# A cross-attention and mixture-of-experts block on one core: buffers of 512 bytes or more begin at multiples of 128 bytes instead of 64

## The chip, the cores and the metric

The kernel runs on one core of a Trainium2 chip. The metric is the device time of one execution in microseconds (us). Each time is the median of several executions. The profile is of one execution, taken by the hardware profiler.

## The reference

The kernel computes a transformer block on x (64 sequences of 64 tokens, 256 features) with a context of the same shape.

```python
x = x + jnp.tanh(g_xattn[0]) * attention(_layernorm(x), ctx_2048, Wq, Wk, Wv, Wo, ...)
x = x + jnp.tanh(g_ffn[0]) * experts(_layernorm(x), w_router, w_gate, w_up, w_down, ...)
```

The attention has 16 query heads and 4 key and value heads of 128, RMS norm and rotary embedding on queries and keys, and keys and values from the 64 context tokens and the 64 own tokens of each sequence. The expert part has a shared expert of width 352, and 8 experts of width 176 of which each token takes the best two by a softmax router, scaled by 2.5.

## The kernel before

**Stages.** The 4096 tokens are 32 tiles of 128 (two sequences each). After an opening of some 49 us (sine and cosine tables, weight loads), attention runs over 128 steps, one for each tile and each of the 4 key and value heads. The steps are staggered by hand: in the step that computes the scores of (tile, head) n, TensorE also projects queries and keys for n + 2 (b_q, L1697, and b_kv, L1711), transposes queries and keys of n (b_qT, b_kT, L1754 and L1758), transposes the softmax of n - 1 (b_pT, L1777), multiplies it by the values (b_aT, L1784) and applies the output projection to n - 2 (b_o, L1795). Then come 71 slots of 128 rows, sorted by expert (L1998 to L2052), and last the shared expert for tiles 8 to 31 (L1828, L1940, L1946). Tiles 0 to 7 of the shared expert run between attention and the slots.

**Matmuls.** The projections and the experts run in fp32r, one pass over the moving columns for each matmul, three matmuls for one product (high by high, high by low, low by high; the tables PASSES and the names _hi and _lo). Scores, values and transposes run in f32. In the profile's names a group b_kv<-w_group,kv_in_hi writes b_kv, streams w_group and holds kv_in_hi as the stationary operand. A b_kv group is 12 matmuls of 256 columns, a b_o group 12 of 256, a b_q group 6 of 512, a gate or up projection 6 of 352, a down projection of the shared expert 9 of 256 and one of a slot 5 of 256.

**Order of the work.** Each engine has its own program, with semaphores between them. ScalarE (ACT) and VectorE (DVE) empty the PSUM banks and write the high and low parts, GpSimd (POOL) does part of the norms and the rotary embedding, SyncE (SP) issues nearly all transfers.

**Memory.** All SBUF buffers are placed by hand. The helper `sb` keeps a cursor in bytes per partition, places a buffer there and moves the cursor on by the size rounded up to 64. With an `at` argument it places the buffer over older ones, from a cursor of its own. The first buffer is at byte 16,512. Rings used in turn matter below: `yS0` to `yS7` hold the normed tokens of shared-expert tile t in yS[t % 8], where tiles 8 and later write their gate to b_q and their up projection to b_kT; `s_in0` to `s_in3` hold a slot's rows, of which 0 and 2 are transposed into b_kT and 1 and 3 into b_o; `s_silu0` is computed from b_q and `s_silu1` from b_kv; `w2_new0` and `w2_new1` are stored to memory in turn. Of the eight chunks sincos0 to sincos7, ScalarE's final steps (L912 to L914) come in the order 0, 4, 1, 5, 2, 6, 3, 7.

Of the kernel before, what the change touches and what calls it, by code (L numbers as in the profile page):

```python
# [63 lines left out]
PI_BELOW = 3.1415925  # L64
PASSES = ((0, 0), (0, 1), (1, 0))
HI, LO = 0, 1

def need(eng, sem, count):
# [28 lines left out]
def flamingo(nc, x, ctxT, posx, posc, invf, g_xattn, g_ffn, q_w, k_w, wq, wkv, wo, wr, wg, wd, out):  # L98
    ctx = ExitStack()
    with ctx:  # L100
# [3 lines left out]
        def sb(name, shape, dt, at=None):  # L104
            size = int(np.prod(shape[1:])) * mybir.dt.size(dt)
            where = cursor if at is None else at
            t = nc.alloc_sbuf_tensor_at(name, shape, dt, offset=where[0])
            where[0] += -(-size // 64) * 64
            return t

        def parts(name, shape, at=None):
            return [sb(f"{name}_{p}", shape, F32R, at) for p in ("hi", "lo")]

        ident = sb("ident", [P, P], F32)
        gates = sb("gates", [P, 2], F32)
        gates_raw = sb("gates_raw", [P, 2], F32)
        minus_half = sb("minus_half", [P, 8], F32)
# [2033 lines left out]
```

How the kernel before makes its waits and increments, by code:

```python
def need(eng, sem, count):  # L69
    if not isinstance(count, int) or count > 0:
        eng.wait_ge(sem, count)
# [346 lines left out]
            def load_inputs(t, p):  # L419
                need(sp, x_normed, t - 1)
                sp.dma_start(x_in[p][:], x[bass.ds(t, 1), :, :].rearrange("a p n -> p (a n)")).then_inc(ld_x[p], 16)
                if isinstance(t, int) and t == 2:
                    sp.wait_ge(ctx_hi, 1)
                need(sp, ctx_lo, t - 2)
                sp.dma_start(ctx_raw[p][:], ctxT[bass.ds(t, 1), :, :, :].rearrange("a p c n -> p (a c) n")) \
                  .then_inc(ld_ctx[p], 16)
# [47 lines left out]
            def load_yS(t):  # L475
                i, r = divmod(t, RING // 2)
                if t >= RING:
                    sp.wait_ge(up_done, t - RING + 1)
                elif t >= RING // 2:
                    sp.wait_ge(q_done, 4 * TILES)
                    sp.wait_ge(kv_done, 4 * TILES)
                need(sp, ld_yS[r], 16 * i)
                sp.wait_ge(st_yT, 16 * (t + 1))
                sp.dma_start(yS_both[t % RING][:].rearrange("p a c n -> p (a c n)").bitcast(F32),
                             yT_dram[t, :, :]).then_inc(ld_yS[r], 16)
# [1 line left out]
            def load_x1_first():  # L487
                for p in range(2):
                    sp.wait_ge(st_x1[p], 16 * (PAIRS - 1))
                for n, (read, times) in enumerate(((x_normed, TILES), (ctx_lo, TILES - 1))):
                    sp.wait_ge(read, times)
# [1185 lines left out]
        @block.tensor  # L1678
        def _(pe):
            pe.wait_ge(consts_set, 9)
```

## Time and profile before

| what | value |
|---|---|
| median of 3 executions | 1233.44 us |
| lowest and highest | 1232.87 and 1234.34 us |
| the profiled execution | 1232.5 us |
| its span (first to last instruction) | 1230.7 us |
| granted TensorE clock, mean | 0.999 of full speed |

In the views, PE is TensorE's matmul, PEld its weight loads (which overlap), DVE VectorE, ACT ScalarE, POOL GpSimd, and SPq the transfers that SyncE issues. The chain is the work that ended last, followed back from the last instruction to what released each step. In order of time, each of its pieces has a start, a length that counts the piece's share of the chain, and a number of instructions, so that the length over the number is the pace at which they follow one another. The duration of one matmul in other views is longer than that, since matmuls are pipelined.

### The profile page before, as it was taken

The page shows a single profiled execution, that of the slowest core. Times are in us where ns is not written, and L with a number is a line of the kernel's source. Part 1 is how long each engine was busy: PE and PEld are TensorE (multiplying, and loading weights), DVE is VectorE, ACT ScalarE, POOL GpSimd, SP SyncE. Part 2 cuts the span into 40 slices and gives each one's busy share as a digit, 9 for nine tenths or more (in the row PEclk, how much of TensorE's full clock was granted, in tenths as well). Part 3 has the DMA queues.
Part 4 walks back from the last instruction along what each step waited for, and adds up shares of the span by engine and source line. Part 5 has one row for each costly group of instructions (what it writes and reads, how often), then busy time and mean ns, then how long its engine had stood idle before and what let it go on. Part 6 is the DMA issues. An engine that isn't in the chain of part 4 may idle for free.

```text
span 1230.7 us, 31490 instructions
## 1 busy us (share of the span) xinstructions
PE 1205.3 (98%) x8781; PEld 1137.3 (92%) x8782; DVE 1008.7 (82%) x2992; ACT 884.9 (72%) x3754; POOL 922.4 (75%) x1124
## 2 busy tenths in 40 slices
PE   6899999999999999999999999999999999999998
PEld 3688999999999999999999999999999999999997
DVE  8788888888888888888888888888888677777443
ACT  7978777777777777777777777777777546666322
POOL 2778888888888888888888888888887425556654
PEclk9999999999999999999999999999999999999999
DMA  6634233322222222223333333222236536554575
GB/s 179 198 115 128 72 111 106 100 90 90 90 90 90 94 90 94 90 90 93 115 108 99 103 103 120 94 75 75 75 110 213 193 104 188 163 158 150 186 230 158
DMA packets 128792, 148.57 MB, mean 121 GB/s; under 512 B 13824, under 2 KB 108288, under 8 KB 127968
## 3 DMA queue, kind: packets, MB, share of 16 engines
q1 hardware_dynamic: 122256, 130.16, 34.8%
q0 software_dynamic: 6480, 17.77, 4.0%
q8 instruction: 22, 0.36, 0.1%
q14 instruction: 34, 0.28, 0.1%
HBM read 66.93 MB, written 80.76 MB: 120 GB/s over the span
## 4 chain that ended last, share of the span: by engine, by line
PE 94%; DVE 2%; ACT 2%; issue 1%; DMA 0%; SPq 0%; DVEq 0%
PE b_kv L1711 14%; PE b_q L1697 14%; PE b_o L1795 13%; PE b_sc L1769 9%; PE b_aT L1784 9%; PE b_pT L1777 5%; PE b_qT L1758 4%; PE b_q L2031 3%; PE b_kv L2031 3%; PE b_q L1828 2%; PE b_kT L1754 2%; PE b_kT L1828 2%; PE b_aT L1946 1%; PE b_aT L2048 1%; PE b_pT L2048 1%; PE b_o L1747 1%
## 5 line engine op out<-in xcount | busy, mean ns | idle before, releaser
L1711 PE MATMUL b_kv<-w_group,kv_in_hi 128*128 128x256 f32 x992 | 205.6, 305 | 0.0
L957 ACT ACTIVATE probs<-b_sc,neg_max 128x128 f32<-128x128 f32 x512 | 180.5, 372 | 0.1
L747 POOL TENSOR_TENSOR qk_r<-qk_me,minus_half 128x6 f32<-128x6 f32 x128 | 172.8, 1350 | 10.1
L751 POOL TENSOR_TENSOR q_rot<-q_rot,q_sin 128x512 f32<-128x512 f32 x128 | 164.4, 1284 | 6.7 <-DVE q_sin L1273 1.9
L1711 PEld LDWEIGHTS b_kv<-w_group,kv_in_hi 128*128 128x128 f32 x992 | 161.8, 190 | 6.7 <-issue 0.4
L1697 PE MATMUL b_q<-w_group,kv_in_hi 128*128 128x512 f32 x496 | 164.8, 413 | 0.0
L951 ACT ACTIVATE pT<-b_pT 128x512 f32<-128x512 f32 x128 | 76.7, 600 | 99.7 <-PE b_pT L1777 97.7
L1795 PE MATMUL b_o<-wo_hi,aT_hi 128*128 128x256 f32 x480 | 143.5, 299 | 0.1
L1769 PE MATMUL b_sc<-kT,qT 128*128 128x128 f32 x1024 | 135.9, 275 | 6.8 <-ACT qT L946 4.9
L754 POOL TENSOR_TENSOR q_rot<-q_rot,qk_r 128x512 f32<-128x512 f32 x128 | 133.7, 1044 | 10.0
L1711 PE MATMUL b_kv<-w_group,kv_in_lo 128*128 128x256 f32 x496 | 139.6, 282 | 0.0
L940 ACT ACTIVATE junk<-b_q 128x128 bf16<-128x128 f32 x512 | 133.9, 283 | 0.0
L1769 PEld LDWEIGHTS b_sc<-kT,qT 128*128 128x128 f32 x1024 | 124.7, 191 | 9.0 <-issue 8.1
L1795 PE MATMUL b_o<-wo_lo,aT_hi 128*128 128x256 f32 x480 | 133.0, 277 | 0.0
L1795 PE MATMUL b_o<-wo_hi,aT_lo 128*128 128x256 f32 x480 | 132.7, 276 | 0.0
L1784 PE MATMUL b_aT<-pT,v 128*128 128x256 f32 x512 | 131.4, 379 | 0.0
L745 POOL TENSOR_TENSOR qk_me<-qk_ms,eps_rms 128x6 f32<-128x6 f32 x128 | 32.2, 252 | 119.0 <-ACT junk L928 118.7
L1283 DVE TENSOR_REDUCE neg_max<-b_sc 128x4 f32<-128x512 f32 x128 | 88.3, 690 | 36.6 <-PE b_sc L1769 34.7
L1784 PEld LDWEIGHTS b_aT<-pT,v 128*128 128x128 f32 x512 | 96.5, 189 | 17.5 <-issue 0.5
L940 ACT ACTIVATION_READ_ACCUMULATOR junk<-b_q 128x1 f32 x512 | 111.2, 217 | 0.0
L957 ACT ACTIVATION_READ_ACCUMULATOR probs<-b_sc,neg_max 128x1 f32 x512 | 109.1, 213 | 0.0
L760 POOL TENSOR_TENSOR k_rot<-k_rot,k_sin 128x256 f32<-128x256 f32 x128 | 93.6, 731 | 11.4 <-DVE k_sin L1259 8.8
(309 smaller groups left out, 3937.5 us busy)
## 6 DMA issues: line engine op xcount, KB each, us to landing
xs_scratch<-zeros SPq DMA_DIRECT2D x34, 1032.0 KB, 6.3
s_in<-xs_scratch SPq DMA_DIRECT2D x71, 129.0 KB
yT_scratch<-yT SPq DMA_DIRECT2D x32, 256.0 KB
yS<-yT_scratch SPq DMA_DIRECT2D x32, 256.0 KB, 3.0
routed<-ys_scratch SPq DMA_DIRECT2D x32, 256.0 KB, 3.5
w_hi_all<-w_scratch SPq DMA_DIRECT2D x3, 1536.0 KB, 13.6
x_in<-in_x SPq DMA_DIRECT2D x32, 128.0 KB, 2.3
ctx_raw<-in_ctxT SPq DMA_DIRECT2D x32, 128.0 KB, 2.5
```

The lines of the kernel that those rows point to most:

```text
L747: nc.gpsimd.tensor_tensor(qk_r[g % 2][:], qk_me[:], minus_half[:, 0:REP + NB], ALU.pow).then_inc(r_ready, 1)
L751: nc.gpsimd.tensor_tensor(q_rot[g % 2][:], q_rot[g % 2][:], q_sin[g % 2][:], ALU.add) \
L754: nc.gpsimd.tensor_tensor(q_rot[g % 2][:], q_rot[g % 2][:], qk_r[g % 2][:, 0:REP].unsqueeze(2).to_broadcast([P, REP, HD]), ALU.mult) \
L760: nc.gpsimd.tensor_tensor(k_rot[g % 2][:], k_rot[g % 2][:], k_sin[g % 2][:], ALU.add) \
L940: last = nc.scalar.activation(junk[:, h, :], b_q[:, h * HD:(h + 1) * HD], ACT.Square, scale=HD ** -0.5, accum_out=qk_ms[g % 2][:, h:h + 1])
L957: last = nc.scalar.activation(probs[:, j, :], b_sc[:, j * P:(j + 1) * P], ACT.Exp, bias=neg_max[g % 2][:, j:j + 1], accum_out=row_sum[g % ...
L1283: nc.vector.tensor_reduce(neg_max[g % 2][:], b_sc[:].rearrange("p (j n) -> p j n", j=REP), AX.X, ALU.max, negate=True).then_inc(max_ready, 1)
L1697: last = nc.tensor.matmul(b_q[:], kv_in[p][a][:, c, 1:3, :], wq_of(b, gg)[:, c, :], start=(c == 0 and (a, b) == PASSES[0]), stop=(c == DC ...
L1711: last = nc.tensor.matmul(b_kv[:, s * 2 * HD:(s + 1) * 2 * HD], kv_in[p][a][:, c, 2 * s:2 * s + 2, :], wkv_of(b, c)[:, g % KVH, :], start= ...
L1769: last = nc.tensor.matmul(b_sc[:, o:o + P], qT[:, s, 2 * j:2 * j + 2, :], kT[:, s, :], start=True, stop=True)
L1784: last = nc.tensor.matmul(b_aT[:, s * REP * S:(s + 1) * REP * S], v_s[g % KVH][:, s, :], pT[:, s, :], start=True, stop=True)
L1795: last = nc.tensor.matmul(b_o[:, 0:D], aT[a][:, h, :, :], wo_s[b][:, gg * REP + h, :], start=(gg == 0 and h == 0 and (a, b) == PASSES[0]), ...
```

## The change

```
+WIDE, LINE = 512, 128
...
             size = int(np.prod(shape[1:])) * mybir.dt.size(dt)
             where = cursor if at is None else at
+            if size >= WIDE:
+                where[0] = -(-where[0] // LINE) * LINE
             t = nc.alloc_sbuf_tensor_at(name, shape, dt, offset=where[0])
             where[0] += -(-size // 64) * 64
```

A buffer of 512 bytes or more per partition first rounds its cursor up to a multiple of 128. The first that this moves is wg_raw, at 18,240. The addresses below follow from the sizes, in the order of the calls of `sb` (bytes; in brackets the rest modulo 128):

| buffers | before | after |
|---|---|---|
| ident | 16,512 (0) | 16,512 (0) |
| wr (128 bytes) | 18,112 (64) | 18,112 (64) |
| wg_raw, wg_lo, wq_raw | 18,240 (64) | 18,304 (0) |
| wd_raw, wd_lo | 46,400 (64) | 46,464 (0) |
| w_group, w2_hi_all | 65,856 (64) | 65,920 (0) |
| sincos2 | 59,456 (64) | 59,520 (0) |
| wo_hi, x1_most / wo_lo | 115,008 / 131,392 (64) | 115,072 / 131,456 (0) |
| hid0 to hT1_lo | 150,592 to 158,272 (64) | 150,656 to 158,336 (0) |
| x_in, x_res, x1_out, x_n | 160,064 to 168,256 (64) | 160,128 to 168,320 (0) |
| s_silu0 / s_silu1 | 164,160 (64) / 164,864 (0) | 164,224 (0) / 164,992 (0) |
| kv_in0_hi to kv_in1_lo, yS4 to yS7 | 169,280 to 175,424 (64) | 169,344 to 175,488 (0) |
| s_in0, s_in2 | 177,472, 179,648 (64) | 177,536, 179,840 (0) |
| s_in1, s_in3 | 178,560, 180,736 (0) | 178,688, 180,992 (0) |
| q_rot0 to v3, qT, kT, probs, pT | 179,328 to 200,832 (0) | 128 more (0) |
| sT, s_hid, s_hT, s_out | 181,824 to 195,136 (64) | 320 more (0) |
| sincos0, sincos4 | 195,712, 199,808 (0) | 128 more (0) |
| aT_hi, aT_lo | 202,880, 204,928 (0) | 203,008, 205,056 (0) |
| y_row0 / y_row1 | 207,360 (0) / 209,472 (64) | 207,488 (0) / 209,664 (0) |
| yT0, yT1 | 211,584, 213,632 (0) | 256 more (0) |
| w2_new0, w2_new1, yS0 to yS3 | 219,648 to 225,792 (0) | 384 more (0) |

All slices of the weights that a matmul streams are whole multiples of 128 bytes from their buffer's start, and so are the stationary slices. The last byte used goes from 227,840 to 228,224 (229,368 are there).

## Rows read from the trace of the kernel before

**Rows 1.** The page: busy time, share and instructions of each engine.
```profile
PE 1205.3 (98%) x8781; PEld 1137.3 (92%) x8782; DVE 1008.7 (82%) x2992; ACT 884.9 (72%) x3754; POOL 922.4 (75%) x1124
```

**Rows 2.** Busy us in windows: PE, PEld, DVE, ACT, POOL, clock, transfers.
```profile
0.00:49.00 49.00, 33.65 (x123) 20.35 (x125) 38.57 (x79) 41.37 (x122) 20.81 (x41) 1.00 0.80 236
49.00:1143.00 1094.00, 1089.77 (x8075) 1035.84 (x8074) 933.52 (x2839) 819.12 (x3583) 852.19 (x1017) 1.00 0.35 109
500.00:909.00 409.00, 409.00 (x3064) 388.35 (x3064) 358.39 (x1020) 316.93 (x1467) 345.87 (x394) 1.00 0.30 94
1143.00:1230.70 87.70, 81.93 (x588) 81.15 (x586) 36.56 (x76) 24.45 (x52) 49.45 (x67) 0.98 0.62 199
```

**Rows 3.** The page: the chain that ended last, shares of the span.
```profile
PE 94%; DVE 2%; ACT 2%; issue 1%; DMA 0%; SPq 0%; DVEq 0%
```

**Rows 4.** The chain in order of time, one step of attention.
```profile
601.04 1.37 PE b_o L1795 x12
602.42 0.89 PE b_sc L1769 x8
...
603.96 1.38 PE b_q L1697 x6
605.34 0.86 PE b_aT L1784 x4
606.21 1.43 PE b_kv L1711 x12
```

**Rows 5.** Single buffers: operations on s_silu, y_row and s_in, ns min/median/max.
```profile
L1118 ACT ACTIVATE s_silu<-b_q x36: 309/318/347, 999.2 to 1141.8; 128x176 f32<-128x176 f32 x36
L1118 ACT ACTIVATE s_silu<-b_kv x35: 310/318/318, 1001.8 to 1139.8; 128x176 f32<-128x176 f32 x35
...
L1322 DVE TENSOR_SCALAR y_row<-x_out,ln_mv,ln_rstd x32: 536/539/558, 79.0 to 980.5; 128x512 f32<-128x512 f32 x32
L1998 PE MATMUL b_kT<-ident,s_in x72: 270/272/273, 996.2 to 1137.8; 128*128 128x128 f32 x72
L1998 PE MATMUL b_o<-ident,s_in x70: 271/272/273, 997.9 to 1135.5; 128*128 128x128 f32 x70
```

**Rows 6.** The chain in order of time, the closing stage.
```profile
1142.00 0.36 PE b_aT L2048 x3
...
1146.85 0.96 PE b_q L1828 x6
1147.81 0.96 PE b_kT L1828 x6
1148.78 1.08 PE b_sc L1946 x9
...
1156.84 0.97 PE b_q L1828 x6
1157.81 0.95 PE b_kT L1828 x6
...
1166.84 0.97 PE b_q L1828 x6
```

**Rows 7.** ScalarE in order of time, the opening.
```profile
15.10 0.71 ACT L914 ACTIVATE sincos<-sincos,half_pi 128x512 f32<-128x512 f32 x1
...
25.03 0.70 ACT L914 ACTIVATE sincos<-sincos,half_pi 128x512 f32<-128x512 f32 x1
```

**Rows 8.** Waits: who for whom, us in total, times, longest.
```profile
POOL qk_me L745 <- ACT junk L928: 118.7, 67, 15.8
...
PE b_sc L1769 <- ACT qT L946: 4.9, 3, 2.5
```

**Rows 9.** Landing of w2_new's stores (100 to 200 us), then of the output tiles' stores.
```profile
DMA to landing us min/median/max: 2.3/2.3/2.3
DMA to landing us min/median/max: 1.7/2.1/4.0
```

**Rows 10.** The page: groups of b_kv and b_o matmuls, with counts.
```profile
L1711 PE MATMUL b_kv<-w_group,kv_in_hi 128*128 128x256 f32 x992 | 205.6, 305 | 0.0
...
L1795 PE MATMUL b_o<-wo_hi,aT_hi 128*128 128x256 f32 x480 | 143.5, 299 | 0.1
```

More of the change, by code:

```diff
@@ L66 @@
 HI, LO = 0, 1
+WIDE, LINE = 512, 128
 def need(eng, sem, count):
@@ L106, in sb @@
             where = cursor if at is None else at
+            if size >= WIDE:
+                where[0] = -(-where[0] // LINE) * LINE
             t = nc.alloc_sbuf_tensor_at(name, shape, dt, offset=where[0])
```

## The prediction

> **What bounds the kernel now.** I read the busy shares first [rows 1], then the busy time in windows [rows 2], then the chain of work that ended last, as a share by line [rows 3] and in order of time [rows 4, 6], and the list of waits [rows 8]. The reader is to see one engine. TensorE is busy for 1205.3 of 1230.7 us [rows 1]. In windows it is idle for 15.4 us of the first 49 us, for 5.8 us of the last 88 us, and for 4.2 us in all of the 1094 us between [rows 2]. The chain is 94% TensorE and 0% DMA [rows 3]. The long wait totals in [rows 8] belong to GpSimd, ScalarE and VectorE, which wait for TensorE or for each other with slack; the longest of TensorE's own that I show is 4.9 us over three times. So a change of memory addresses can move the time only if (a) it changes how fast TensorE's matmuls and weight loads follow one another, or (b) it changes the ScalarE and VectorE work in the first 49 us. Nothing else is worth more than a few tenths of a microsecond.
>
> **What the change does.** It adds and removes no instruction, wait or transfer. It moves addresses (the table in the section on the change): the weights, the kv_in ring, the trig tables, hT, sT and s_hT go from 64 bytes past a multiple of 128 ("phase 64" below) to phase 0. What was at phase 0 already (ident, q_rot, qT, kT, v, probs, pT, aT, yT, yS0 to yS3, s_in1, s_in3, s_silu1, the w2_new pair) stays at phase 0 and moves by whole multiples of 128, or not at all. So the kernel before already runs both phases side by side, and its trace holds the comparison.
>
> **Part 1: ScalarE and VectorE, and the first 49 us.** s_silu0 is at phase 64 and fed from b_q, s_silu1 at phase 0 from b_kv. ScalarE's write takes 318 ns in both [rows 5]. For VectorE, the row on y_row covers y_row0 (phase 0) and y_row1 (phase 64) together, and its 32 instructions spread from 536 ns to 539 (median) to 558 [rows 5]: half of them could not be off by more than 22 ns. In the opening, ScalarE's last step for chunk 2 of sincos, at phase 64, takes 0.70 us at 25.03, and that for chunk 4, at phase 0, takes 0.71 us at 15.10 [rows 7]. Taken at zero. The bounds: 0.01 us less or more on each of a few sincos steps that are on the chain, below 0.1 us either way. GpSimd shows no pair of phases that I can separate. In [rows 2] it has slack in every stage (345.9 busy of 409 us in the second half of attention), and no wait of TensorE for it is among the long ones [rows 8], so it is hidden behind TensorE's queue of work; if it lost all slack, that would need 18% on every one of its instructions.
>
> **Part 2: transposes and f32 matmuls.** The 72 transposes of s_in0 and s_in2 (phase 64, into b_kT) and the 70 of s_in1 and s_in3 (phase 0, into b_o) both take 272 ns [rows 5]. The cost is zero for these and, by them, for the other transposes whose input moves (x_n, y_row1, hid, s_hid). Scores, values and the transposes of attention have both operands at phase 0 before and after.
>
> **Part 3: the fp32r matmuls.** These carry the chain, and here one comparison is missing: every fp32r moving operand (w_group, wo, w2_hi_all, wg_lo, wd_lo; wr too, which is too small to be moved) is at phase 64 before, so no row shows one at phase 0. The stationary operand does come in both phases. In the closing stage each token tile of the shared expert reads yS[t % 8]: t = 9 to 11 read yS1 to yS3 (phase 0), t = 12 to 15 read yS4 to yS7 (phase 64). A tile starts every 3.33 us in both. Its two groups of six take 0.96 + 0.96 us at phase 0 and 0.97 + 0.95 us at phase 64: the sum is 1.92 in both [rows 6]. Three tiles take 9.99 us (1146.85 to 1156.84) and the next three 10.00. The split between the two groups does shift by 0.01 us, so addresses are visible to TensorE, but the sum is not: 0.1% of the stage. Taken over the whole kernel, that is at most 1.2 us either way.
>
> What disturbs this is that two groups of identical form do not run alike. The twelve matmuls of b_kv (kv_in at phase 64 against w_group at 64) take 1.43 us, 119 ns each. The twelve of b_o (aT at phase 0 against wo at 64) take 1.37 us, 114 ns each [rows 4]. Both have 128x256 moving and 128x128 stationary. The nine of the shared down projection (hT at 64, wd at 64) take 1.08 us, 120 ns each, in a stage where ScalarE and VectorE do little [rows 2, 6], so it isn't traffic from those that slows them. Something in the addresses makes 5 ns. Phase is one candidate. A higher address bit is another: every fp32r moving operand of the groups at 119 to 120 ns lies below byte 115,008 of the partition, both halves of wo lie above it, and no buffer changes sides by being moved 64 to 384 bytes. The yS comparison argues for the second, as it shows no effect of phase; but it is at 352 columns. My value is zero; the ends are the two rivals.
>
> **What a rule would make of it.** The Trainium skill ("SBUF — State Buffer", on the DMA port swizzle) says that SBUF works in lines of 16 bytes and that only a change of line costs; 64 is a multiple of 16, so by that rule all phases are alike and the sum is zero. It doesn't explain the 114 against 119 ns, so I don't rest on it.
>
> **Part 4: transfers.** Stores of w2_new alternate between a buffer at a multiple of 256 and one at 128 past it, and land in 2.3 us, minimum, median and maximum alike [rows 9]. x1_out, x1_most and s_out go from 64 to 128 past a multiple of 256. None of these is waited for except the last output tile, which lands in about 2 us [rows 9] after the last VectorE step. By that rule the last store would be 6% slower in its transfer part, an estimate of 0.1 us if all of its 2.1 us were that; the trace has no such difference between 0 and 128 past. Taken at zero from the rows.
>
> **The sum.** 0 (part 1) + 0 (part 2) + 0 (part 3) + 0 (part 4). The profiled execution took 1232.5 us, 1.8 of it outside the span; the median of three runs is 1233.44, and the sum is made to that: 1233.4 us.
>
> **Rivals.**
> *Faster, phase of the stationary operand.* If phase 0 is what gives aT its 114 ns, then kv_in, hT and s_hT gain it: 1488 matmuls of b_kv (992 that hold kv_in_hi [rows 10], and half as many that hold kv_in_lo) by 5 ns (7.4 us); 32 x 9 = 288 of the shared down projection and 71 x 5 = 355 of the slots' (0.36 us for the first three [rows 6], 120 ns each) by 6 ns (3.9 us). Sum 11.3 us, 1222.1 us. For it: four families agree. Against it: yS. Its far end is that the moving operand at phase 64 is the cause and every fp32r matmul reaches the column rate of the f32 ones: 0.86 us for four of 256 columns with two passes [rows 4], 107.5 ns a pass, or the 111 ns of the b_sc pairs (0.89 us for 8) where weight loads bound it. That gives 744 x (230 - 215) = 11.2 us for b_q (124 groups of 6, 1.38 us each [rows 4]), 12.2 for b_kv, 4.6 for b_o, 810 x 12 = 9.7 for the 352-column ones (0.96 or 0.97 us for six, 160 ns, against 148), 5.8 for down: 43.5 us, 1190 us. Nothing speaks for it but that it hasn't been seen.
> *Slower, phases that meet.* If a matmul is slow where stationary and moving operand have the same phase, b_kv, hT and s_hT are slow for that and b_o is fast because aT (0) and wo (64) differ. The change puts both at 0. Then 1440 matmuls of b_o (three times 480 [rows 10]) go from 114 to 119 ns: 7.2 us, 1240.6 us. It decides from 1.7 ns a matmul on (0.2%). For it: the same four families, equally well. Against it: yS0 to yS3 against w2 differ in phase, yS4 to yS7 do not, and both cost 1.92 us.
> *No effect, since it doesn't do what it says.* It does move the buffers: the first one of 512 bytes after the small ones is at 18,240, and 18,240 is 142.5 x 128. This isn't apart from the forecast in time.
>
> **How the numbers follow.** Forecast (zero, with up to 1.2 us of re-timing either way): 0.64, own range 1231 to 1236. Stationary phase: 0.14, 1222. Full column rate: 0.03, 1190. Phases that meet: 0.14, 1241. Something unseen: 0.05, split between the sides. A measurement of this kernel can tell about 0.2% (2.5 us) from no change. The range of 8 in 10 takes the forecast and the rival on the slow side, and part of the way to the fast one: 1224 to 1242. Of the forecast's 0.64, 0.03 lies beyond 2.5 us on each side. Faster 0.14 + 0.03 + 0.02 + 0.03 = 0.22; slower 0.14 + 0.03 + 0.03 = 0.20; same 0.58.
>
> **What would show it.** In the changed kernel's trace: b_kv groups of 12 still at 1.43 us, b_o groups at 1.37, b_q groups of 6 at 1.38, down projections at 1.08 for nine, shared tiles every 3.33 us. A b_o group at 1.43 shows that phases that meet are the cause; b_kv at 1.37 and down at 1.03 show the stationary phase; b_q at 1.29 the full rate. I'm wrong if any of these groups moves by 0.03 us or more, since attention has 120 to 124 of each, or if TensorE gets waits that [rows 8] don't have.

## The result and the profile after

The changed kernel takes 1238.15 us (median of 8, 1237.34 to 1239.27) where the kernel before took 1233.59 us (median of 8, 1232.41 to 1234.44) beside it: slower by 4.6 us, ratio 1.0037 with a 95% interval of 1.0027 to 1.0048. The profiled execution took 1238.04 us with a span of 1236.3 us, 5.6 us longer than the span before. The diff adds three lines, so line n of the kernel before is line n + 3 here.

The page of the changed kernel first: busy times of the engines and the chain's shares, to be read beside [rows 1] and [rows 3].

```profile
PE 1211.1 (98%) x8781; PEld 1142.7 (92%) x8782; DVE 1007.2 (81%) x2992; ACT 884.2 (72%) x3754; POOL 918.1 (74%) x1124
...
PE 93%; DVE 2%; ACT 2%; DMA 1%; issue 1%; SPq 0%; POOL 0%; DVEq 0%; POOLq 0%
```

TensorE is busy for 5.8 us more with the same 8781 matmuls; the three other engines are busy for slightly less. So no other engine's own work got longer: the matmuls themselves take longer. The granted clock isn't the cause. It is 1.00 in attention, as it was before [rows 2] (window in us, then PE, PEld, DVE, ACT, POOL, clock, transfers):

```profile
110.00:977.00 867.00, 863.85 (x6413) 818.45 (x6412) 749.25 (x2132) 664.74 (x3069) 715.74 (x818) 1.00 0.33 103
```

The waits hardly change. The three longest of TensorE's waits in the changed kernel (us in total, times, longest):

```profile
PE b_kT L1688 <- DVE x_n L1238: 8.3, 2, 8.0
PE b_sc L1772 <- ACT qT L949: 4.4, 3, 2.5
PE b_kT L1757 <- POOL k_rot L763: 2.4, 2, 1.8
```

The first was 8.3 us before too, and the second 4.9 us [rows 8]. The third was one wait of 1.9 us before; the second wait in it, of 0.6 us, is new. Next, where in the execution it happens: the first and last start of the matmuls of the output projection, then of the transposes of the slots. First the kernel before, then the changed one (duration of one in ns, min/median/max, then the starts in us).

```profile
L1795 PE MATMUL b_o<-wo_lo,aT_hi x480: 276/276/283, 110.0 to 977.5; 128*128 128x256 f32 x160
```

```profile
L1798 PE MATMUL b_o<-wo_lo,aT_hi x480: 278/282/287, 110.1 to 983.7; 128*128 128x256 f32 x160
L2001 PE MATMUL b_kT<-ident,s_in x72: 270/273/273, 1002.5 to 1143.7; 128*128 128x128 f32 x72
```

At 110 us the two kernels are level. At the last output projection the changed one is 6.2 us late (983.7 against 977.5), at the first slot 6.3 us (1002.5 against 996.2 [rows 5]), at the last slot transpose 5.9 us, and at the end 5.6 us. The loss is made in attention, but not all of it by the pace. The lateness grows at an even rate until 958 us (on the clock of the kernel before), from 0.1 to 5.5 us. Right after that comes the new wait of 0.6 us: TensorE waits for GpSimd's k_rot, which comes after a long transfer. Two pieces of the chain of the changed kernel there (start, length, in us):

```profile
961.69 6.89 DMA xs_scratch<-y_row,row_i
968.64 0.92 POOL k_rot L763
```

About as much is given back in the slots, so at the end the lateness is what the even growth had made. The same wait of 0.6 us stands in one of the runs below in which every pace is that of before (all_plus_64). So it doesn't come from the pace of the matmuls.

One step of attention, in the chain of the changed kernel (start, length, both in us), beside [rows 4]:

```profile
604.16 1.42 PE b_o L1798 x12
605.58 0.89 PE b_sc L1772 x8
...
607.13 1.40 PE b_q L1700 x6
608.52 0.86 PE b_aT L1787 x4
609.39 1.43 PE b_kv L1714 x12
```

b_o went from 1.37 to 1.42 us, b_q from 1.38 to 1.40. b_kv, b_sc and b_aT stand where they stood. From the starts of the matmuls in all groups, the median time from a b_o group's first start to the next group's is 1458 ns before and 1501 after, and for b_q 1468 and 1478 ns: 43 and 10 ns a group. b_o's 43 ns aren't in every group: 12 of the 120 were already longer before, and little or nothing is added to them. Summed over the groups up to 958 us, b_o adds 4.5 us, b_q 1.3 and b_kv -0.1, together 5.6 us, beside the 5.4 us by which the lateness grows there. The timeline shows the pace. First a b_o group's second half before, then after (starts in us):

```profile
608.71 0.28 PE L1795 MATMUL b_o<-wo_hi,aT_lo 128*128 128x256 f32 x1
...
609.39 0.28 PE L1795 MATMUL b_o<-wo_hi,aT_lo 128*128 128x256 f32 x1
```

```profile
604.59 0.29 PE L1798 MATMUL b_o<-wo_hi,aT_lo 128*128 128x256 f32 x1
...
605.30 0.28 PE L1798 MATMUL b_o<-wo_hi,aT_lo 128*128 128x256 f32 x1
```

Six matmuls take 0.68 us before and 0.71 after. Over all groups this pace (twelfth start less sixth, by six) is 113.3 ns before, in every one of the 120 groups, and 119.4 ns on average after, with none of the 120 groups near 113. In b_kv it is 119.4 before and 119.2 after, with none of 124 groups near 113 in either. This measure, a group's pace, is worked out from the starts in the trace, and the experiments below are read by it.

The closing stage, now that yS0 to yS7 and w2 are all at multiples of 128, in the chain of the changed kernel:

```profile
1155.67 0.96 PE b_q L1831 x6
1156.63 0.95 PE b_kT L1831 x6
1157.58 1.08 PE b_kv L1949 x9
...
1158.99 0.97 PE b_q L1831 x6
```

The second b_q row starts 3.32 us after the first. A tile starts every 3.32 to 3.33 us through this stage, as before the change [rows 6].

### The profile page after: what moved, and what is told of

It reads as the page before. It is cut to its first block, busy times and chain, and to the rows that moved or that the text cites. A ratio compares the mean times of both kernels' runs of the same rounds, so it can differ in the third digit from the quotient of the medians.

```text
span 1236.3 us, 31490 instructions
## 1 busy us (share of the span) xinstructions
PE 1211.1 (98%) x8781; PEld 1142.7 (92%) x8782; DVE 1007.2 (81%) x2992; ACT 884.2 (72%) x3754; POOL 918.1 (74%) x1124
## 4 chain that ended last, share of the span: by engine, by line
PE 93%; DVE 2%; ACT 2%; DMA 1%; issue 1%; SPq 0%; POOL 0%; DVEq 0%; POOLq 0%
PE b_kv L1714 14%; PE b_q L1700 14%; PE b_o L1798 13%; PE b_sc L1772 9%; PE b_aT L1787 9%; PE b_pT L1780 5%; PE b_qT L1761 4%; PE b_q L2034 3%; PE b_kv L2034 3%; PE b_kT L1757 2%; PE b_q L1831 2%; PE b_kT L1831 2%; PE b_aT L1949 1%; PE b_pT L2051 1%; PE b_aT L2051 1%; PE b_o L1750 1%
## 5 line engine op out<-in xcount | busy, mean ns | idle before, releaser
L1798 PE MATMUL b_o<-wo_hi,aT_lo 128*128 128x256 f32 x480 | 135.4, 282 | 0.0
```

The source lines that it names most:

```text
L1798: last = nc.tensor.matmul(b_o[:, 0:D], aT[a][:, h, :, :], wo_s[b][:, gg * REP + h, :], start=(gg == 0 and h == 0 and (a, b) == PASSES[0]), ...
```

## The experiments

All twelve kernels have the instructions of one of the two kernels and differ in addresses alone. The edit is one line in `sb`, ahead of the call that places the buffer, and a table of bytes to skip before a buffer:

```
+PAD = {...}
...
             where = cursor if at is None else at
+            where[0] += PAD.get(name, 0)
             t = nc.alloc_sbuf_tensor_at(name, shape, dt, offset=where[0])
```

What lies above a skipped gap moves with it, unless the next entry fills the move up to 256 bytes (to 64 in aT_plus_32). Places below are counted in steps of 64 bytes modulo 256: before, wo is at place 1 and aT at 2, w_group at 1 and kv_in at 1; after, wo is at 2, aT at 0, w_group and kv_in at 2. The distance of a pair is odd or even by these places. The time of the kernel before is that of the same chip. The column for 119 to 120 ns holds groups from 118.3 to 120.0 ns, with an average of 119.0 to 120.0 in each b_o row, so it lies close to 117.8; between 113.5 and 117 ns there is no group.

| run | wo, aT | b_o groups at 113.3 / 117.8 / 119 to 120 ns | w_group, kv_in | b_kv groups | us, against before |
|---|---|---|---|---|---|
| before | 1, 2 odd | 120 / 0 / 0 | 1, 1 even | 0 / 0 / 124 | |
| after | 2, 0 even | 0 / 0 / 120 | 2, 2 even | 0 / 0 / 124 | 1238.15, 1233.59 |
| aT_to_64 | 1, 3 even | 0 / 0 / 120 | 1, 1 even | 0 / 0 / 124 | 1238.22, 1233.04 |
| above_wo_plus_64 | 2, 3 odd | 3 / 117 / 0 | 1, 2 odd | 102 / 22 / 0 | 1233.05, 1233.04 |
| after_aT_to_64 | 2, 1 odd | 117 / 3 / 0 | 2, 2 even | 0 / 0 / 124 | 1233.43, 1233.04 |
| kv_in_64_and_128 | 1, 0 odd | 0 / 120 / 0 | 1, 2 odd and 1, 3 even | 49 / 11 / 64 | 1235.83, 1233.04 |
| aT_plus_256 | 1, 2 odd | 119 / 1 / 0 | 1, 1 even | 0 / 0 / 124 | 1232.12, 1232.84 |
| wo_0_aT_192 | 0, 3 odd | 15 / 105 / 0 | 1, 0 odd | 16 / 108 / 0 | 1233.33, 1232.84 |
| aT_plus_32 | 1, 2.5 | 0 / 4 / 116 | 1, 1 even | 0 / 0 / 124 | 1242.00, 1232.84 |
| both_pairs_good | 1, 2 odd | 101 / 19 / 0 | 1, 2 odd | 52 / 72 / 0 | 1233.19, 1232.84 |
| all_plus_64 | 2, 3 odd | 119 / 1 / 0 | 2, 2 even | 0 / 0 / 124 | 1231.13, 1230.99 |
| q_k_rot_plus_64 | 1, 2 odd | 85 / 35 / 0 | 1, 1 even | 0 / 0 / 124 | 1231.98, 1230.99 |
| wo_plus_64 | 2, 2 even | 0 / 0 / 120 | 1, 1 even | 0 / 0 / 124 | 1237.52, 1230.99 |
| from_q_rot_plus_64 | 1, 3 even | 0 / 0 / 120 | 1, 1 even | 0 / 0 / 124 | 1237.18, 1230.99 |

**One part alone: aT.** `PAD = {'aT_hi': 64}` on the kernel before.

> The kernel before, with only aT (hi and lo) moved up by 64 bytes, so that aT and wo are both 64 past a multiple of 128; what lies above aT moves by 64 too, all else stays. Theory A (a 256-column fp32r matmul is slow where stationary and moving operand have the same rest modulo 128): the group of 12 b_o matmuls goes from 1.37 to about 1.42 us, and the kernel to about 1238, 4 to 6 us slower than before. Theory B (what costs is that wo, the streamed operand, begins at a multiple of 128): wo isn't moved, so b_o stays at 1.37 us and the time at 1233.6. Theory C (no relation, a re-timing by chance of the whole layout): no forecast, any value from 1.37 to 1.43. b_kv stays at 1.43 us by all.

1238.22 us against 1233.04, ratio 1.0039 (1.0022 to 1.0056). b_o is at 119.0 ns on average, with no group near 113. One buffer pair (and what lies above it) moved by 64 bytes makes a loss as large as that of the change, and it does so with wo, and every other weight, where it was. Theory B falls.

**The pair kept, its surroundings moved.** `PAD = {'wo_hi': 64}` on the kernel before.

> The kernel before, with everything from wo upwards moved up by 64 bytes; the weights below wo (w_group, w2, wg_lo, wd_lo) stay at 64 past a multiple of 128. aT against wo keeps its relation (64 apart modulo 128) with both absolute places swapped; kv_in against w_group, hT and s_hT against w2 and wd come to be 64 apart where they were 0 apart. Theory A (same rest modulo 128 is slow): b_o stays at 1.37 us, b_kv falls from 1.43 to 1.37 us, the nine of the shared down projection from 1.08 to about 1.03 us, so 7 + 2 to 4 us faster than before, about 1223. Theory B (streamed operand at a multiple of 128 is slow): b_o goes to 1.42 us and the time to about 1238. Theory B' (stationary operand at a multiple of 128 is fast): b_kv falls but b_o rises, about 1229.

1233.05 against 1233.04 us, 1.0007 (0.9997 to 1.0017): neither theory's number. b_kv did as theory A said in 102 groups. But b_o, at the odd distance it had before, went to a third pace, 117.8 ns. In the chain of this run (start, length, in us):

```profile
604.12 1.40 PE b_q L1697 x6
606.38 1.37 PE b_kv L1711 x12
608.41 1.42 PE b_o L1795 x12
```

b_kv takes 1.37 us here and b_o 1.42, the reverse of [rows 4]. Summed over the groups, b_kv gains 5.9 us, b_o loses 4.8 and b_q 1.5, so gain and loss cancel. Theory A in its first form (odd is fast) falls; what is left of it is that an even distance is slow.

The third family of 256 columns speaks against "odd is fast" even more. The shared down projection (hT against w2 and wd) is at an odd distance here and was expected at about 1.03 us for nine:

```profile
1152.58 1.06 PE b_kv L1946 x9
```

That is 118.9 ns from start to start (ninth start less third, by six) against 120.3 before. In the four layouts that bring hT to an odd distance (this one, wo_0_aT_192, both_pairs_good, wo_plus_64) it runs at 118.9 to 119.8 ns, in the others at 120.2 to 120.5, and no full group of nine comes near 113. So the fast pace is a matter of b_o and b_kv; why the down projection doesn't take it is open.

**The change, with aT put back to an odd distance.** `PAD = {'aT_hi': 64, 'aT_lo': -64}` on the changed kernel, after its rounding (the second entry undoes the rounding of aT_lo).

> The changed kernel, with only aT (hi and lo) moved to 64 past a multiple of 128, so that aT and wo are 64 apart again, with wo at a multiple of 128. Theory A (same rest modulo 128 is slow): b_o falls back from 1.42 to 1.37 us, and the kernel from 1238.2 to about 1233. Theory B (wo at a multiple of 128 is slow): b_o stays at 1.42 us and the time at 1238.

1233.43 against 1233.04 us, 1.0003 (0.9993 to 1.0013), with b_o at 113.3 ns in 117 groups. The loss is gone although wo and the other weights stand at multiples of 128, as after the change. Two neighbouring groups in its chain (start, length, in us; here, too, the rounding's lines and one more shift the line numbers, so that L1799 is b_o's):

```profile
601.10 1.37 PE b_o L1799 x12
...
608.35 1.37 PE b_o L1799 x12
```

Both take the 1.37 us that b_o took before the change [rows 4].

**Odd and even in one execution.** `PAD = {'kv_in0_hi': 64, 'kv_in1_hi': 64}` on the kernel before.

> The kernel before, with kv_in0 (hi and lo, even tiles) moved up by 64 bytes and kv_in1 (odd tiles) by 128, so that within one execution b_kv's groups alternate in fours between operands 64 apart and 128 apart; sT and s_hT move by 128, aT by 128 (it stays 64 apart from wo modulo 128, though 192 instead of 64 modulo 256). Theory A (same rest modulo 128 is slow): the b_kv groups of even tiles fall from 1.43 to 1.37 us, those of odd tiles stay at 1.43; b_o stays at 1.37; the kernel is 62 x 0.06 = 3.7 us faster. Theory A modulo 256 (only 0 apart is slow): both fall, 7 us faster. Theory B (it is the place of the streamed operand): nothing changes.

1235.83 against 1233.04 us, 1.0025 (1.0015 to 1.0035), slower where a gain was expected. The b_kv groups do alternate in fours: of the 60 on even tiles (odd distance) 49 run at 113.3 to 113.5 and 11 at 117.8 ns, of the 64 on odd tiles (128 bytes apart) all at 118.5 to 120.0. Two neighbouring b_kv groups in the chain of this run:

```profile
607.99 1.42 PE b_kv L1711 x12
...
615.29 1.38 PE b_kv L1711 x12
```

The one is of a tile 128 bytes apart, the other of a tile 64 bytes apart. So 128 bytes apart is slow like 0 apart. The kernel loses all the same since b_o, which stayed at an odd distance, is at 117.8 ns in all 120 groups.

**The period.** `PAD = {'aT_hi': 256}`.

> What the first four runs left: counted in places of 64 bytes modulo 256, the fast b_o groups had (wo, aT) at (1, 2) and (2, 1), the slow ones at (2, 0), (1, 3), (2, 3) and (1, 0), so 64 apart modulo 128 is not enough. Here only aT moves, by 256 bytes. Theory P (what counts is the pair of places modulo 256): b_o stays at 1.37 us and the kernel at 1233. Theory Q (a longer period, 512 bytes or more, or no period): b_o goes to 1.42 and the kernel to 1238.

1232.12 us in one execution (before 1232.84), b_o at 113.3 ns in 119 of 120 groups. Moving aT by 256 bytes changes nothing that shows; theory Q falls.

**Another odd pair.** `PAD = {'wo_hi': 192, 'aT_hi': 128}`.

> The kernel before with everything from wo upwards moved by 192 bytes and aT by 320, so that wo is at place 0 and aT at place 3 (of 64 bytes, modulo 256), which no run had. Theory P with the rule that the places must be each other's complement (sum 3: 1 with 2, 2 with 1, 0 with 3): b_o stays fast at 1.37 us. Theory P without such a rule, two good pairs by chance: b_o at 1.42. b_kv (w_group at 1, kv_in at 0) stays slow at 1.42 to 1.43 by both.

b_o is at 117.8 ns in 105 groups and at 113.3 in 15. The rule of complements falls. The time, 1233.33 us, partly hides it, since b_kv (now at an odd distance too, which the expectation had overlooked when it said that b_kv stays slow) gives back 2.2 us of the 3.8 that b_o loses; by the last b_o the run is 1.8 us late.

**Half a step.** `PAD = {'aT_hi': 32, 'neg_max0': 32}`.

> The kernel before with only aT moved, by 32 bytes. If the pace follows the place in steps of 64 bytes alone (half of what a matmul loads then lies in the next place), b_o lies between, about 1.39 to 1.40 us; if a start at a multiple of 64 matters of itself, b_o goes beyond 1.43 us.

Nearer to the second: the piece in the chain is 1.44 us. From the first start of a group to that of the next group it is 1515 ns, against 1501 after the change, and the time is 1242.00 us against 1232.84 in one execution. b_o in the chain of this run:

```profile
605.46 1.44 PE b_o L1795 x12
```

A pair 96 bytes apart (modulo 256) isn't half good; its pace is 119.1 ns in all but the first and the last three groups, and its groups are the longest but one of all runs. Of the 9.2 us, b_o's groups make 6.1 in sum. Another 0.95 us is there before the first of them, and 1.7 come after attention; neither is traced to a cause.

**Both pairs at the places that wo and aT have before.** `PAD = {'kv_in0_hi': 64, 'junk': 192, 'hT0_hi': 64}`.

> The kernel before with kv_in, hT, sT and s_hT moved by 64 bytes to place 2 (of 64 bytes, modulo 256) against weights at place 1, which is the pair that wo and aT have before, and aT moved by 256, which keeps its pair. Theory P: b_kv falls from 1.43 to 1.37 us in all 124 groups, the shared down projection from 1.08 to 1.06 us, and b_o stays at 1.37: 7 us less, b_q may give 1 to 2 us back as in the run with everything above wo moved by 64; about 1227.5. Theory Q: b_kv falls and b_o rises, about 1232.

1233.19 against 1232.84 us, 1.0002 (0.9993 to 1.0011). Not the 5 us hoped for: b_kv is fast in 52 of 124 groups only, b_o lost 19 of its 120, and b_q's groups went from 1468 to 1485 ns. So the same pair of places is fast in every b_o group of the kernel before and in four of ten b_kv groups here. The places of the pair allow the fast pace and don't ensure it. The b_q groups, whose kv_in and w_group are at an odd distance here, gain nothing from it at 512 columns. The shared down projection takes 1.08 us, not the 1.06 expected.

**Everything moved.** `PAD = {'ident': 64}` on the kernel before.

> The kernel before with every buffer moved by 64 bytes, ident included: all distances are kept, all absolute places change, and the weights, kv_in, hT and wo come to multiples of 128 as in the changed kernel. Theory R (only distances count: the pair a matmul streams and loads, and the distances in the matmuls just before it, which set how the group starts): b_o stays at 1.37 us in all 120 groups and the time at 1233, although wo and all weights are at multiples of 128. Theory S (absolute places count too): b_o changes in part or in all, up to 1238. The run with all above wo moved by 64 kept the pair of b_o but not its distance to ident and w_group, and had b_o at 117.8 ns a matmul in 117 of 120 groups.

1231.13 against 1230.99 us, 1.0001 (0.9991 to 1.0010). b_o is at 113.3 ns in 119 groups, b_kv at 119.4 on average, the groups' medians are those of before (1458 and 1616 ns), and all weights are at multiples of 128, as in the changed kernel. So a shift by 64 bytes common to all buffers counts for nothing: distances count. Beside above_wo_plus_64, which has wo, aT, q_rot and kv_in at these very places and ident and w_group 64 bytes lower, it shows that b_o's pace depends on buffers that b_o itself doesn't read.

**Only what comes before b_o moved.** `PAD = {'q_rot0': 64, 'v0': 192}`.

> The kernel before with only the buffers that TensorE transposes just before b_o moved by 64 (q_rot, q_sin, k_rot, k_sin), and v and all above by 256, which keeps their places. The pair of b_o keeps its places modulo 256. Theory R (the group's start decides between the two paces of an odd pair, 113.3 and 117.8 ns): many b_o groups change to 117.8 ns a matmul, 1.41 us, and the kernel to 1234 to 1238. Theory R' (the start doesn't matter, only the absolute places of the pair): b_o stays at 1.37 us in all groups and the kernel at 1233.

85 groups at 113.3 and 35 at 117.8 ns; 1231.98 us against 1230.99 in one execution, a smaller loss than the expectation had. Two neighbouring groups of the same form and buffers (each head streams its own slice of wo, 4096 bytes from the last), in the chain of this run:

```profile
507.09 1.42 PE b_o L1795 x12
...
514.32 1.38 PE b_o L1795 x12
```

and their second halves in its timeline:

```profile
507.52 0.28 PE L1795 MATMUL b_o<-wo_hi,aT_lo 128*128 128x256 f32 x1
...
508.23 0.28 PE L1795 MATMUL b_o<-wo_hi,aT_lo 128*128 128x256 f32 x1
...
514.75 0.28 PE L1795 MATMUL b_o<-wo_hi,aT_lo 128*128 128x256 f32 x1
...
515.43 0.28 PE L1795 MATMUL b_o<-wo_hi,aT_lo 128*128 128x256 f32 x1
```

0.71 and 0.68 us for six. Theory R' falls: b_o's own pair kept its places, and its pace changed. Theory R's forecast of the pace came true, but its reason, the start, is argued and not shown. In most groups of either kind the last transposes and the first two b_o matmuls start at the same distances within 1 ns; they part from the third matmul on. And 28 of the 35 groups at 117.8 ns belong to one of the four heads, which has only 2 at 113.3, so the step counts besides. v to pT moved by 256 bytes in this run too, which no run did alone.

**The other one alone: wo.** `PAD = {'wo_hi': 64, 'w_cos': 192}`.

> The kernel before with only wo moved by 64 bytes, and all above it by 256: aT and wo are 0 apart modulo 128. Even distances are slow: b_o at about 119 ns a matmul, 1.42 us, in all 120 groups, kernel at 1238, as when aT alone was moved. If wo must be moved together with aT for a loss: 1233.

1237.52 us against 1230.99 in one execution, b_o at 120.0 ns on average, with no group near 113. Moving either one of the pair by 64 bytes loses. Here silu, hid and hT moved by 64 as well, but they are used outside b_o's steps almost throughout, and b_o's groups show the loss themselves (184.5 us in sum against 178.0).

**Even, with another start.** `PAD = {'q_rot0': 64}`.

> The kernel before with everything from q_rot upwards (aT included) moved by 64, so that b_o's pair is at an even distance (128 apart modulo 256) and the transposes before it are moved too. If an even distance can't be fast whatever the start: no b_o group at 113 ns, all at about 119, kernel at 1238, b_kv unchanged. If a changed start can make it fast: some groups at 113 ns.

1237.18 us against 1230.99 in one execution, b_o at 119.4 ns on average, none at 113. In the four layouts with wo and aT at an even distance, in the one 32 bytes off, and in all with w_group and kv_in at an even distance, not one group was at 113 ns.

## Why the prediction was wrong

The forecast was no change, 1233.4 us, with its own range at 1231 to 1236. Measured were 1238.15 us beside 1233.59, a loss of 0.37% and clear of the noise. The range of 8 in 10, 1224 to 1242, holds the result only because it took in the rival on the slow side; 0.58 stood on "same" and 0.20 on "slower".

- *What bounds the kernel*: right. The loss is TensorE's pace. The idle time and the waits stayed, but for one wait of 0.6 us for GpSimd, which the prediction had called hidden; it is given back before the end.
- *Part 1, ScalarE and VectorE at zero; Part 2, transposes at zero*: right as far as the trace shows. At 110 us the kernels are level, and the transposes take 272 or 273 ns.
- *Part 4, transfers at zero*: right for the total. The profiled execution lies 1.7 us over its span after and 1.8 before. Near the end of attention one transfer stands in the chain that did not before (0.8% of that stretch), with the wait of 0.6 us behind it.
- *Part 3 is the step that failed*: it took the term for b_o at zero, in its sentence "The yS comparison argues for the second, as it shows no effect of phase; but it is at 352 columns". The comparison was sound at 352 columns: in the changed kernel, where all eight yS are at an even distance, a tile still starts every 3.33 us. It doesn't carry to 256 columns, where b_o's groups show 43 ns in the median (1.37 to 1.42 us, 113.3 to 119.4 ns a matmul). The forecast leant on it against four families at 256 columns, b_o and b_kv among them. It also leaned to "a higher address bit" for the 5 ns between b_o and b_kv. No run supports that: b_kv, with w_group below byte 115,008, reaches 113.3 ns in 102 groups as soon as kv_in is 64 bytes off.
- *The rival "phases that meet" (0.14)* had the place and the sign. Its size was 1440 x 5 ns = 7.2 us. Measured were 4.6 us on b_o in sum (43 ns a group or 3.6 ns a matmul in the median, since the start of a group costs nearly the same in both), plus 1.3 us on b_q that no rival had. Its other half, that b_kv is slow because kv_in and w_group meet, was right too. For hT it was wrong: the shared down projection at an odd distance still runs at 118.9 to 119.8 ns. So only two of the "four families" that spoke for it follow it; the slots' down projection was not read. Its rule, 64 apart is fast, was too simple: an odd distance ran at 113.3 or 117.8 ns.
- *The rival of the stationary phase* (0.14) is excluded: kv_in, hT and s_hT came to phase 0 and b_kv stayed at 1.43 us; aT_to_64 is slow and after_aT_to_64 fast, both with aT at phase 64. *Full column rate* (0.03) is excluded too: b_q rose. Its "two passes" for an f32 matmul is a reading of 215 ns for 256 columns; no run here takes passes apart.

Of the Trainium skill's rule in Part 3 ("SBUF — State Buffer", lines of 16 bytes), these runs show the limit: all places compared here are multiples of 16, and the pace differs by 5 to 6%.

What stays open: why an odd distance has two paces and what picks one; why the shared down projection doesn't follow; and the 10 ns a group on b_q, whose own pair kept its distance of 0. Six of them lie in the step from its last matmul to b_aT's first (230 ns before in most groups, 236 after). The traces narrow that down. The step is 236 ns in three layouts alone, after, after_aT_to_64 and from_q_rot_plus_64, and 228 to 234 in most groups of the others, aT_to_64 and q_k_rot_plus_64 among them. So it isn't aT nor q_rot to k_sin, and what from_q_rot_plus_64 moved besides is v, qT, kT, probs and pT, of which b_aT reads pT and v. They weren't moved alone. In above_wo_plus_64 they and kv_in moved together, and the step stays at 229 ns.

## What to carry to other kernels

When fp32r matmuls follow one another without idle time, the distance in SBUF between what a matmul streams and what is loaded can matter. In b_o and b_kv, two buffers at a distance of an even number of 64-byte steps cost 5 to 6% more a matmul at 256 columns (119.0 to 120.0 ns against 113.3); in the shared down projection it was 1%, and at 352 columns nothing showed. So don't expect a gain from rounding all buffers to the same large multiple. Look at the pace per group of matmuls (length by count, in the chain) and compare groups of one shape: two groups of one form at 114 and 119 ns were the sign of it here. An odd distance isn't enough either, so measure the layout. And don't carry a comparison from one shape to another when another family at the disputed shape is in the same trace and says otherwise.

## What the runs showed of the hardware

- In b_o and b_kv, groups of twelve fp32r matmuls of 256 columns, three paces appear: 113.3, 117.8, or 119 to 120 ns. The first never comes with the streamed and the stationary operand an even number of 64-byte steps apart: 0 and 128 bytes apart give the third, in all of 480 b_o groups of four layouts, and aT moved by 32 bytes gives 119.1 ns in 116 of 120. At an odd number it is 113.3 or 117.8.
- The shared down projection, also 256 columns, is at 118.9 to 119.8 ns at an odd distance and 120.2 to 120.5 at an even one.
- Moving all of SBUF's buffers by 64 bytes changes none of these paces and no time (ratio 1.0001); moving aT alone by 256 doesn't either (119 of 120 groups, one execution).
- With b_o's own pair left at its places, moving other buffers turned 35 of 120 groups from 113.3 to 117.8 ns within one execution, 28 of them of one head. What in the step picks the pace isn't shown.
- At 352 columns the closing stage keeps its 3.32 to 3.33 us a tile at either distance, and the f32 groups b_sc and b_aT keep 0.89 and 0.86 us.
